# Moving half of one slot's scaling from VectorE to ScalarE, and the first pair of products behind the first half of the sums

## The chip, the cores and the metric

The kernel runs on one core of one Trainium2 chip. The metric is the time of one execution on the device, in microseconds. Engines are named as in the profile: PE is TensorE's matmul stream, PEld its weight loads, DVE is VectorE, ACT is ScalarE, POOL is GpSimd, SP is SyncE.

## The reference

A graph of 3,125 nodes and 103,125 edges goes through two graph layers, each with a residual and a layer norm. The first is a graph convolution; the change does not touch it. The second is an attention layer over edges with a message and an attention logit for each of 16 x 16 channels, and all that matters here is in these lines:

```
w_m = (efeat @ W_msg + b_msg).reshape(E, in_f, -1)
w_a = (efeat @ W_attn + b_attn).reshape(E, in_f, -1)
h_src = feat[src][:, :, None]
e1 = w_m * h_src
e2 = w_a * h_src
seg_max = segment_max(e2, dst)
ex = exp(e2 - seg_max[dst]);  denom = segment_sum(ex, dst)
ft = segment_sum(e1 * ex / denom[dst], dst).sum(axis=1)
```

## The kernel before

The second layer is the "edge part". Nodes lie 128 to a tile, one to a partition, in 25 tiles. The edges of a tile's nodes are handled in units: a unit takes 8 edges (slots 0 to 7) of each of the 128 nodes. A running maximum and running sums (`acc`) go from unit to unit; when a tile ends, its quotient is formed. There are 116 units, one after the other, and all engines run their own loop over them, four units to a pass, tied by semaphores.

For unit u the work is this. The weights of an edge are a product of its 16 features, split into bfloat16 terms, with a weight matrix: 8 slots x 512 columns of float32 in PSUM. `turn` (L789) transposes the terms on PE, in two halves; `turned` (L997) copies each half to SBUF on ACT. `product` k (L807), k = 0 to 3, makes the 512 columns of slots 2k and 2k+1. PSUM has room for four slots only (`pw`, four banks): products 0 and 2 write banks 0 and 1, products 1 and 3 write banks 2 and 3. Each slot's 512 columns are 16 blocks of 32, and block c is multiplied by channel c of the neighbour's features (`nbr`): that is the scaling, which empties PSUM into `eo`. DVE does it for slots 0 to 5 (`scaled`, L1471, three instructions of two slots); ACT does it for slots 6 and 7 (`last_pair`, L1021, one activation for each block, 32 in all). Then DVE takes the maximum (`peaks`, L1486 to L1505), ACT the exponential (`powers`, L1010), DVE multiplies (`weighted`, L1514), PE sums the 8 slots over an identity matrix in two halves (`sums`, L816 and L820), and DVE takes the sums out (`accumulate`, L1521).

The engines work on different units at a time. In one pass u,

- PE does: sums(u) first half; product 1 of unit u+3; sums(u) second half; turn half 0 of u+4; product 2 of u+3; turn half 1 of u+4; product 3 of u+3; product 0 of u+4.
- ACT does: `high` of u+4 (L982, L984); `last_pair` of u+2; `middle` of u+4 (L991); `fading` (L1002, L1004) and `powers` of u+1; `turned` halves 0 and 1 of u+4.
- DVE does: weighted(u); `rest_one` (L1452) of u+4; peaks of u+1, with the quotient of a tile that has ended (L1532 to L1541); `rest_two` (L1459) of u+4; scaled of u+3; accumulate(u).
- POOL gathers, as soon as `last_pair` of u+2 is done, the neighbours of unit u+6 (L626, eight indirect DMAs), and then the edge features of a later unit (L620).

The waits that matter: product 1 of u+3 waits for `last_pair` of u+2 (`s_pair1_act`), since both use banks 2 and 3; product 0 waits for the third instruction of `scaled` (`s_scaled`); product 2 waits for the first instruction of `scaled`; `last_pair` waits for product 3 (`s_w_act`).

Of the kernel before, what the change touches and what calls it, by code (L numbers as in the profile page):

```python
# [6 lines left out]
P = 128  # L7
# [6 lines left out]
ACT = mybir.ActivationFunctionType  # L14
# [5 lines left out]
FEAT = 16  # L20
HID = 64
CH = FEAT * FEAT
# [7 lines left out]
SETS = 4  # L30
RING = 4
LEAD = 4
# [28 lines left out]
def gnn_kernel(nc, x, src, dst, edge_attr, W1, b1, W2, b2, W3, b3, W_msg, b_msg, W_attn, b_attn, out):  # L61
# [9 lines left out]
    with ExitStack() as ctx:  # L71
        def sb(name, shape, dt=F32, stack=ctx):
            return stack.enter_context(nc.sbuf_tensor(name, shape, dt))

        def sem(name):
            return ctx.enter_context(nc.semaphore(name))
# [142 lines left out]
        nbr = sb("nbr", [P, SETS, SLOT * FEAT])  # L219
# [4 lines left out]
        eo = sb("eo", [P, RING, SLOT * 2 * CH])  # L224
# [14 lines left out]
        pw = ctx.enter_context(nc.psum_tensor("pw", [P, 4, 512], F32))  # L239
# [73 lines left out]
        s_settled_act = sem("s_settled_act")  # L313
# [4 lines left out]
        s_scaled = sem("s_scaled")  # L318
        s_attr = [sem(f"s_attr{b}") for b in range(SETS)]
        s_attr_ok = sem("s_attr_ok")  # L320
        s_attr_free = sem("s_attr_free")
# [6 lines left out]
        s_tT = sem("s_tT")  # L328
# [3 lines left out]
        s_pair0_free = sem("s_pair0_free")  # L332
        s_pair1_dve = sem("s_pair1_dve")
        s_pair1_act = sem("s_pair1_act")
        s_d = sem("s_d")
        s_ex = sem("s_ex")
        s_md = sem("s_md")
# [33 lines left out]
        block = ctx.enter_context(nc.Block())  # L371
# [268 lines left out]
        def _(pe):  # L640
# [117 lines left out]
            for layer in range(3):  # L758
# [4 lines left out]
                with pe.Fori(0, np_) as _p:  # L763
                    c = pe.snap(plane, min_val=0, max_val=MANY)
# [17 lines left out]
            def turn(unit, half, seen):  # L782

                if half == 0:
                    pe.wait_ge(s_lo, seen + 1)
                pe.wait_ge(s_tTc, seen * 2 + half + 1)
                pe.sem_inc(s_settled_pe, 1)
                for j in range(4):
                    mm = pe.matmul(pt[0:KROWS, j * P:(j + 1) * P], terms[:, unit, half * 4 + j, :], identb[:],  # L789
                                   start=True, stop=True)  # L790
                mm.then_inc(s_tT, 1)

            def product(unit, k, seen):

                pe.wait_ge(s_tTc, seen * 2 + k // 2 + 2)
                if k == 0:
                    pe.wait_ge(s_scaled, seen + SETS)
                elif k == 2:
                    pe.wait_ge(s_pair0_free, seen + 1)
                elif k == 1:  # L800
                    pe.wait_ge(s_pair1_act, seen + SETS)
                else:
                    pe.wait_ge(s_pair1_dve, seen + 1)
                pe.sem_inc(s_settled_pe, 1)
                for j in range(2):
                    lo = (2 * k + j) * P
                    mm = pe.matmul(pw[:, 2 * (k % 2) + j, :], termsT[:, unit, lo:lo + P], wk[:], start=True, stop=True)  # L807
                mm.then_inc(s_w_act if k == 3 else s_w, 1)

            def sums(ring, half, seen):  # L810

                total = pair[:, ring % 2, :]
                if half == 0:
                    pe.wait_ge(s_accd, seen + 1)
                    pe.sem_inc(s_settled_pe, 1)
                    pe.matmul(total, ident[:], acc[:], start=True, stop=False, skip_group_check=True)  # L816
                pe.wait_ge(s_p, seen * 2 + half + 1)
# [11 lines left out]
            for u in range(3):  # L829
                for half in range(2):  # L830
                    turn((u + 1) % 2, half, u + 1)
                for k in range(4):
                    product(u % 2, k, u)
            product(1, 0, 3)
            before_last = pe.value_load(levels[0:1, NT + 1:NT + 2], min_val=1, max_val=MANY)

            def pe_unit(b, u, ahead):

                sums(b % RING, 0, u)
                if ahead > 2:  # L840
                    product((b + 3) % 2, 1, u + 3)
                sums(b % RING, 1, u)
                if ahead > 3:
                    turn(b % 2, 0, u + LEAD)
                if ahead > 2:
                    product((b + 3) % 2, 2, u + 3)
                if ahead > 3:
                    turn(b % 2, 1, u + LEAD)
                if ahead > 2:
                    product((b + 3) % 2, 3, u + 3)  # L850
                if ahead > 3:
                    product(b % 2, 0, u + LEAD)

            with pe.Fori(0, before_last) as i:
                for b in range(SETS):
# [5 lines left out]
        def _(act):  # L861
# [71 lines left out]
            for layer in range(3):  # L933
# [8 lines left out]
                with act.Fori(0, np_) as _p:  # L942
                    c = act.snap(plane, min_val=0, max_val=MANY)
# [67 lines left out]

            def last_pair(ring, held, seen):

                act.wait_ge(s_nbr_ok, seen + 1)
                act.wait_ge(s_w_act, seen + 1)
                act.sem_inc(s_settled_act, 1)
                wide = 2 * FEAT
                for j in range(SLOT - 2, SLOT):
                    for c in range(FEAT):
                        lo = j * 2 * CH + c * wide  # L1020
                        done = act.activation(eo[:, ring, lo:lo + wide], pw[:, j - 4, c * wide:(c + 1) * wide], ACT.Copy,  # L1021
                                              scale=nbr[:, held, j * FEAT + c:j * FEAT + c + 1])
                done.then_inc(s_pair1_act, 1)

            act.wait_ge(s_stage, 1)
# [39 lines left out]
        def _(dve):  # L1065
# [10 lines left out]
                      s_g3_free, s_accd):  # L1076
                dve.sem_inc(s, 1)
            dve.sem_inc(s_g3, 2)
            for s in (s_scaled, s_attr_free, s_tT, s_pair1_act):
                dve.sem_inc(s, 4)  # L1080
            dve.sem_inc(s_tTc, 1)
            dve.sem_inc(s_recw, 16)
# [272 lines left out]
            for layer in range(3):  # L1355
# [8 lines left out]
                with dve.Fori(0, np_) as p:  # L1364
                    c = dve.snap(plane, min_val=0, max_val=MANY)
# [44 lines left out]
            wide = [P, NG, FEAT]  # L1410
# [53 lines left out]
            def scaled(ring, held, seen):  # L1464

                dve.wait_ge(s_nbr_ok, seen + 1)
                for k in range(3):
                    dve.wait_ge(s_w, seen * 3 + k + 1)
                    dve.sem_inc(s_settled_dve, 1)
                    h_src = nbr[:, bass.ds(held, 1), 2 * k * FEAT:(2 * k + 2) * FEAT].rearrange("p u c -> p (u c)")  # L1470
                    dve.tensor_tensor(eo[:, bass.ds(ring, 1), k * 4 * CH:(k + 1) * 4 * CH]  # L1471
                                      .rearrange("p r (c f) -> p (r c) f", f=2 * FEAT),
                                      pw[:, 2 * (k % 2):2 * (k % 2) + 2, :].rearrange("p b (c f) -> p (b c) f", f=2 * FEAT),
                                      h_src.unsqueeze(2).broadcast_to([P, 2 * FEAT, 2 * FEAT]),
                                      ALU.mult).then_inc((s_pair0_free, s_pair1_dve, s_scaled)[k], 1)

            def peaks(ring, first, old, new, seen, ended=None):
# [184 lines left out]
```

## Time and profile before

| what | value |
|---|---|
| three timed runs | 2610.61, 2631.48, 2644.78 us; median 2631.48 us |
| span of the profiled execution | 2618.5 us (13 us under the median) |
| mean granted TensorE clock over the span | 0.897 |
| PE, DVE, ACT, POOL busy | 72%, 76%, 56%, 49% of the span |
| first and last `accumulate` of the edge part | 905.9 and 2589.8 us |

The span is the only time of the profiled execution itself, and it lies within the spread of the timed runs. A unit of the edge part takes on average (2589.8 - 905.9) / 114 = 14.8 us.

### The profile page before, as it was taken

Reading aid. Unit: us, or ns where it says so; the run is one execution under the profiler, and the core shown is the slowest. Engines: PE = TensorE matmul, PEld = TensorE weight load, DVE = VectorE, ACT = ScalarE, POOL = GpSimd, SP = SyncE. Lnnn points to the kernel's source line nnn. Section 1 sums busy time; section 2 is a strip of 40 time slices with the busy share of each in tenths; the row PEclk is TensorE's granted clock in tenths of the full one; section 3 lists DMA queues with packets and bytes.
Section 4 is the critical chain, followed back from the end, with each engine's and each line's share of the span. In section 5 each row is a group of like instructions: output and inputs, shape, how many; then the busy total and the mean of one; then the engine's idle time right before and its main releaser. Section 6 shows DMA issues by size and latency. Waiting matters only on the chain.

```text
span 2618.5 us, 37987 instructions
## 1 busy us (share of the span) xinstructions
PE 1880.0 (72%) x5814; PEld 706.3 (27%) x5815; DVE 1989.2 (76%) x3269; ACT 1458.7 (56%) x4999; POOL 1289.6 (49%) x1520
## 2 busy tenths in 40 slices
PE   2445676577982577787887777877888877888855
PEld 1111111132341133233333333333333333333322
DVE  5678999752011588888888888888898898988866
ACT  5124444210001576676777767777776776776643
POOL 2200000425556566656666657666666665666650
PEclk9789989788975699999999989999998998998877
DMA  2000000000001000000000000000000000000000
GB/s 31 17 23 4 0 0 0 2 10 17 11 13 15 9 10 10 9 10 9 10 9 10 9 10 9 10 9 10 9 10 9 10 10 9 9 10 9 9 5 7
DMA packets 85243, 25.74 MB, mean 10 GB/s; under 512 B 61677, under 2 KB 82271, under 8 KB 85087
## 3 DMA queue, kind: packets, MB, share of 16 engines
q0 software_dynamic: 36672, 18.09, 5.7%
q1 hardware_dynamic: 48463, 6.91, 1.8%
q10 hardware_dynamic: 80, 0.43, 0.1%
q14 instruction: 18, 0.15, 0.0%
q8 instruction: 10, 0.16, 0.0%
HBM read 22.73 MB, written 2.51 MB: 10 GB/s over the span
## 4 chain that ended last, share of the span: by engine, by line
issue 29%; DVE 25%; PE 23%; DVEq 17%; ACT 3%; POOL 1%; another core or an unknown queue 1%; DMA 1%; ACTq 0%; POOLq 0%; PEldq 0%; PEld 0%
PE pair L820 9%; DVE eo L1471 6%; DVE hot L1197 4%; DVEq L1490 4%; PE pw L711 3%; DVE eo L1514 2%; DVE eo L1505 2%; PE pw L807 2%; PE pw L708 2%; PE pw L707 2%; DVE top L1486 2%; ACT eo L1021 2%; DVE top L1491 2%; DVE bank L1499 2%; DVEq L1503 1%
## 5 line engine op out<-in xcount | busy, mean ns | idle before, releaser
L626 POOL DMA_INDIRECT nbr<-table,rec x928 | 961.0, 1036 | 527.3 <-ACT eo L1021 274.0
L820 PE MATMUL pair<-eo,ident 128*128 128x512 f32 x1856 | 890.0, 625 | 12.4 <-issue 7.7
L1021 ACT ACTIVATE eo<-pw,nbr 128x32 f32<-128x32 f32 x3712 | 694.3, 371 | 83.1 <-issue 66.9
L1471 DVE TENSOR_TENSOR eo<-pw,nbr 128x1024 f32 (+1 forms) x348 | 412.5, 1218 | 169.3 <-PE pw L807 94.4
L820 PEld LDWEIGHTS pair<-eo,ident 128*128 128x128 f32 x1856 | 366.2, 201 | 494.9 <-issue 479.6
L807 PE MATMUL pw<-wk,termsT 100*128 100x512 bf16 x928 | 307.5, 417 | 249.8 <-issue 173.8
L1197 DVE TENSOR_SCALAR hot<-iota_key,near_key 128x500 bf16<-128x500 f16 x974 | 273.8, 346 | 59.3 <-issue 31.9
L1010 ACT ACTIVATE eo<-eo 128x2048 f32<-128x2048 f32 x116 | 221.5, 1910 | 107.4 <-DVE eo L1505 85.1
L1514 DVE TENSOR_TENSOR eo<-eo x232 | 272.7, 1216 | 5.9 <-issue 4.0
L1505 DVE TENSOR_TENSOR eo<-eo,bank (+1 forms) x116 | 265.3, 2287 | 10.7
L672 PE MATMUL bank<-hot 128*128 128x500 bf16 x488 | 146.7, 414 | 145.4 <-DVE hot L1197 93.1
L997 ACT CAST termsT<-pt 100x512 bf16<-100x512 f32 x232 | 135.5, 584 | 207.3 <-issue 123.4
L789 PE MATMUL pt<-identb,terms 128*100 128x128 bf16 x928 | 99.4, 234 | 171.2 <-issue 83.1
L672 PE MATMUL pair<-hot,x 128*128 128x500 bf16 x474 | 138.3, 412 | 63.5 <-DVE hot L1197 60.4
L807 PEld LDWEIGHTS pw<-wk,termsT 100*128 100x128 bf16 x928 | 68.3, 101 | 409.9 <-issue 409.1
L620 POOL DMA_INDIRECT attr<-in_edge_attr_dram,rec x116 | 115.5, 995 | 98.2 <-issue 57.6
L1486 DVE TENSOR_TENSOR top<-eo 128x1024 f32 (+1 forms) x116 | 141.4, 1219 | 28.2 <-issue 28.2
L789 PEld LDWEIGHTS pt<-identb,terms 128*100 128x100 bf16 x928 | 78.2, 135 | 299.1 <-issue 299.1
L816 PE MATMUL pair<-acc,ident 128*128 128x512 f32 x232 | 145.3, 712 | 5.9 <-DVE acc L1521 4.6
L553 POOL TENSOR_SCALAR place<-place 128x25 f32<-128x25 f32 x1 | 0.4, 387 | 280.9 <-ACTq L958 280.9
L900 ACT CAST counts<-bank 128x500 f32 x79 | 45.5, 576 | 156.0 <-PEq L695 123.8
L900 ACT CAST counts<-pair 128x500 f32 x79 | 45.5, 576 | 141.6 <-PEq L695 130.6
(245 smaller groups left out, 1815.6 us busy)
## 6 DMA issues: line engine op xcount, KB each, us to landing
nbr<-table,rec POOLq DMA_INDIRECT x928
rec<-unit_recs SPq DMA_DIRECT2D x116, 8.0 KB
attr<-in_edge_attr_dram,rec POOLq DMA_INDIRECT x116
unit_recs<-place SPq DMA_DIRECT2D x27, 64.0 KB
shared<-key_row SPq DMA_DIRECT2D x1, 1600.0 KB, 6.7
counts<-in_dst_dram SPq DMA_DIRECT2D x1, 448.0 KB
counts<-in_src_dram SPq DMA_DIRECT2D x1, 448.0 KB
place<-in_src_dram,at_i POOLq DMA_INDIRECT x26, 2.6
```

What stands on the lines that cost most here:

```text
L626: pool.indirect_dma_start(nbr[:, b, j * FEAT:(j + 1) * FEAT], None, table, bass.IndirectOffsetOnAxis(ap=rec[:, b, j:j + 1], axis=0)).then_ ...
L672: return pe.matmul(bank[v][:, 0:NG * WIN], low, hot_key[:, k, :], start=first, stop=False, skip_group_check=True)
L789: mm = pe.matmul(pt[0:KROWS, j * P:(j + 1) * P], terms[:, unit, half * 4 + j, :], identb[:], start=True, stop=True)
L807: mm = pe.matmul(pw[:, 2 * (k % 2) + j, :], termsT[:, unit, lo:lo + P], wk[:], start=True, stop=True)
L820: mm = pe.matmul(total, ident[:], eo[:, ring, j * 2 * CH:(j + 1) * 2 * CH], start=False, stop=(j == SLOT - 1), skip_group_check=True)
L1010: act.activation(here, here, ACT.Exp).then_inc(s_ex, 1)
L1021: done = act.activation(eo[:, ring, lo:lo + wide], pw[:, j - 4, c * wide:(c + 1) * wide], ACT.Copy, scale=nbr[:, held, j * FEAT + c:j * FE ...
L1197: return dve.tensor_scalar(hot_key[:, slot, :].rearrange("p (a d) -> p a d", a=NG), iota_key[:], near_key[v][:, k], None, ALU.is_equal)
L1471: dve.tensor_tensor(eo[:, bass.ds(ring, 1), k * 4 * CH:(k + 1) * 4 * CH] .rearrange("p r (c f) -> p (r c) f", f=2 * FEAT), pw[:, 2 * (k % ...
L1486: dve.tensor_tensor(wide(top4[:]), attention(ring, 0, 4), attention(ring, 4, 8), ALU.max).then_inc(s_attr_free, 1)
L1505: dve.tensor_tensor(here, here, wide(after).unsqueeze(1).broadcast_to([P, SLOT, FEAT, FEAT]), ALU.subtract).then_inc(s_d, 1)
L1514: dve.tensor_tensor(here, here, attention(ring, 4 * half, 4 * half + 4), ALU.mult).then_inc(s_p, 1)
```

## The change

ACT also scales the second half of slot 5 (blocks 8 to 15, from bank 1), ahead of its 32 blocks for slots 6 and 7, and signals that with a new semaphore, `s_half_act`. DVE's third scaling instruction covers one and a half slots in place of two. Product 0 of unit u+3 now also has to wait for ACT's half (banks 0 and 1), and it is moved: from the end of pass u-1 to pass u, between the first half of the sums and product 1. The prologue's extra `product(1, 0, 3)` goes.

```diff
             def product(unit, k, seen):
                 pe.wait_ge(s_tTc, seen * 2 + k // 2 + 2)
                 if k == 0:
                     pe.wait_ge(s_scaled, seen + SETS)
+                    pe.wait_ge(s_half_act, seen + SETS)
...
-            product(1, 0, 3)
...
                 sums(b % RING, 0, u)
                 if ahead > 2:
+                    product((b + 3) % 2, 0, u + 3)
                     product((b + 3) % 2, 1, u + 3)
...
-                if ahead > 3:
-                    product(b % 2, 0, u + LEAD)
...
             def last_pair(ring, held, seen):
+                def block(j, c):
+                    lo = j * 2 * CH + c * wide
+                    return act.activation(eo[:, ring, lo:lo + wide], pw[:, j - 4, c * wide:(c + 1) * wide], ACT.Copy,
+                                          scale=nbr[:, held, j * FEAT + c:j * FEAT + c + 1])
                 act.wait_ge(s_nbr_ok, seen + 1)
+                act.wait_ge(s_scaled, seen + SETS + 1)
+                act.sem_inc(s_settled_act, 1)
+                for c in range(FEAT // 2, FEAT):
+                    done = block(5, c)
+                done.then_inc(s_half_act, 1)
                 act.wait_ge(s_w_act, seen + 1)
                 act.sem_inc(s_settled_act, 1)
                 for j in range(SLOT - 2, SLOT):
                     for c in range(FEAT):
-                        ...
+                        done = block(j, c)
                 done.then_inc(s_pair1_act, 1)
...
                 for k in range(3):
+                    blocks = 2 * FEAT if k < 2 else 3 * FEAT // 2
...
-                                      h_src.unsqueeze(2).broadcast_to([P, 2 * FEAT, 2 * FEAT]),
+                                      h_src.unsqueeze(2).broadcast_to([P, blocks, 2 * FEAT]),
                                       ALU.mult).then_inc((s_pair0_free, s_pair1_dve, s_scaled)[k], 1)
```

## Rows read from the trace of the kernel before

**Rows 1.** The page: busy time by engine, and the chain that ended last

```profile
PE 1880.0 (72%) x5814; PEld 706.3 (27%) x5815; DVE 1989.2 (76%) x3269; ACT 1458.7 (56%) x4999; POOL 1289.6 (49%) x1520
...
issue 29%; DVE 25%; PE 23%; DVEq 17%; ACT 3%; POOL 1%; another core or an unknown queue 1%; DMA 1%; ACTq 0%; POOLq 0%; PEldq 0%; PEld 0%
```

**Rows 2.** Timeline of PE in one pass: start, us, line, operation [idle before]

```profile
1812.11 3.67 PE L820 MATMUL pair<-eo,ident 128*128 128x512 f32 x8
1817.76 0.59 PE L807 MATMUL pw<-wk,termsT 100*128 100x512 bf16 x2 [1.98 <-issue]
1818.19 3.60 PE L820 MATMUL pair<-eo,ident 128*128 128x512 f32 x8
1821.62 0.39 PE L789 MATMUL pt<-identb,terms 128*100 128x128 bf16 x4
...
1822.86 0.40 PE L789 MATMUL pt<-identb,terms 128*100 128x128 bf16 x4 [0.41 <-ACT termsT L997]
...
1824.10 0.59 PE L807 MATMUL pw<-wk,termsT 100*128 100x512 bf16 x2 [0.41 <-issue]
```

**Rows 3.** Timeline of ACT in the same pass, to the next last_pair

```profile
1810.65 5.23 ACT L1021 ACTIVATE eo<-pw,nbr 128x32 f32<-128x32 f32 x28
1816.12 0.82 ACT L1021 ACTIVATE eo<-pw,nbr 128x32 f32<-128x32 f32 x4 [0.24 <-issue]
...
1822.13 0.59 ACT L997 CAST termsT<-pt 100x512 bf16<-100x512 f32 x1 [0.77 <-PE pt L789]
...
1824.56 4.92 ACT L1021 ACTIVATE eo<-pw,nbr 128x32 f32<-128x32 f32 x27
```

**Rows 4.** Timeline of DVE in the same pass: the third scaling instruction

```profile
1822.72 1.23 DVE L1471 TENSOR_TENSOR eo<-pw,nbr 128x1024 f32 x1 [0.93 <-issue]
```

**Rows 5.** Costliest groups: L1021 and L1471 by the page, L1491 by shape

```profile
L1021 ACT ACTIVATE eo<-pw,nbr 128x32 f32<-128x32 f32 x3712 | 694.3, 371 | 83.1 <-issue 66.9
L1471 DVE TENSOR_TENSOR eo<-pw,nbr 128x1024 f32 (+1 forms) x348 | 412.5, 1218 | 169.3 <-PE pw L807 94.4
...
L1491 DVE TENSOR_TENSOR top<-top 128x512 f32<-128x512 f32 x62 | 42.9, 692 | 5.5
```

**Rows 6.** Timeline of POOL: a gather of edge features

```profile
1829.39 0.95 POOL L620 DMA_INDIRECT attr<-in_edge_attr_dram,rec  x1 [0.30 <-issue]
```

**Rows 7.** Timeline of a pass with a tile's end, and the next

```profile
1848.26 0.42 ACT L1002 ACTIVATE mdiff<-mdiff 128x256 f32<-128x256 f32 x1 [3.64 <-DVE mdiff L1501]
...
1850.97 0.40 PE L789 MATMUL pt<-identb,terms 128*100 128x128 bf16 x4 [2.52 <-DVE terms L1459]
...
1855.01 5.82 ACT L1021 ACTIVATE eo<-pw,nbr 128x32 f32<-128x32 f32 x32
...
1861.06 0.60 PE L807 MATMUL pw<-wk,termsT 100*128 100x512 bf16 x2
...
1865.51 0.57 ACT L997 CAST termsT<-pt 100x512 bf16<-100x512 f32 x1
```

**Rows 8.** How often a tile ended and a unit was accumulated

```profile
L1532 DVE RECIPROCAL rden<-pair x25: 1748/1750/1758, 1009.7 to 2599.2; 128x256 f32 x25
...
L1521 DVE TENSOR_TENSOR acc<-pair,fade x115: 677/680/690, 905.9 to 2589.8; 128x512 f32<-128x512 f32 x115
```

**Rows 9.** Timeline of PE in two passes with slow second halves; windows (PEclk eighth)

```profile
1874.67 0.59 PE L807 MATMUL pw<-wk,termsT 100*128 100x512 bf16 x2 [1.87 <-issue]
1875.11 5.29 PE L820 MATMUL pair<-eo,ident 128*128 128x512 f32 x8
...
2415.31 1.01 PE L807 MATMUL pw<-wk,termsT 100*128 100x512 bf16 x2 [3.34 <-ACT eo L1021]
2416.12 6.18 PE L820 MATMUL pair<-eo,ident 128*128 128x512 f32 x8
...
2415.30:2422.30 7.00, 6.99 (x13) 2.96 (x14) 3.23 (x4) 2.69 (x4) 4.82 (x5) 0.57 0.06 5
```

More of the change, by code:

```diff
@@ L334, in gnn_kernel @@
         s_pair1_act = sem("s_pair1_act")
+        s_half_act = sem("s_half_act")
         s_d = sem("s_d")
@@ L1012, in last_pair @@
             def last_pair(ring, held, seen):
-                act.wait_ge(s_nbr_ok, seen + 1)
+                wide = 2 * FEAT
+                def block(j, c):
+                    lo = j * 2 * CH + c * wide
+                    return act.activation(eo[:, ring, lo:lo + wide], pw[:, j - 4, c * wide:(c + 1) * wide], ACT.Copy,
+                                          scale=nbr[:, held, j * FEAT + c:j * FEAT + c + 1])
+                act.wait_ge(s_nbr_ok, seen + 1)
+                act.wait_ge(s_scaled, seen + SETS + 1)
[3 more added lines that the diff above has]
+                done.then_inc(s_half_act, 1)
                 act.wait_ge(s_w_act, seen + 1)
                 act.sem_inc(s_settled_act, 1)
-                wide = 2 * FEAT
                 for j in range(SLOT - 2, SLOT):
                     for c in range(FEAT):
-                        lo = j * 2 * CH + c * wide
-                        done = act.activation(eo[:, ring, lo:lo + wide], pw[:, j - 4, c * wide:(c + 1) * wide], ACT.Copy,
-                                              scale=nbr[:, held, j * FEAT + c:j * FEAT + c + 1])
+                        done = block(j, c)
                 done.then_inc(s_pair1_act, 1)
@@ L1078, in _ @@
             dve.sem_inc(s_g3, 2)
-            for s in (s_scaled, s_attr_free, s_tT, s_pair1_act):
+            for s in (s_scaled, s_attr_free, s_tT, s_pair1_act, s_half_act):
                 dve.sem_inc(s, 4)
@@ L1469, in scaled @@
                     dve.sem_inc(s_settled_dve, 1)
-                    h_src = nbr[:, bass.ds(held, 1), 2 * k * FEAT:(2 * k + 2) * FEAT].rearrange("p u c -> p (u c)")
-                    dve.tensor_tensor(eo[:, bass.ds(ring, 1), k * 4 * CH:(k + 1) * 4 * CH]
+                    blocks = 2 * FEAT if k < 2 else 3 * FEAT // 2
+                    h_src = nbr[:, bass.ds(held, 1), 2 * k * FEAT:2 * k * FEAT + blocks].rearrange("p u c -> p (u c)")
+                    dve.tensor_tensor(eo[:, bass.ds(ring, 1), k * 4 * CH:k * 4 * CH + blocks * 2 * FEAT]
                                       .rearrange("p r (c f) -> p (r c) f", f=2 * FEAT),
-                                      pw[:, 2 * (k % 2):2 * (k % 2) + 2, :].rearrange("p b (c f) -> p (b c) f", f=2 * FEAT),
-                                      h_src.unsqueeze(2).broadcast_to([P, 2 * FEAT, 2 * FEAT]),
+                                      pw[:, 2 * (k % 2):2 * (k % 2) + 2, :].rearrange("p b (c f) -> p (b c) f", f=2 * FEAT)
+                                      [:, 0:blocks, :],
+                                      h_src.unsqueeze(2).broadcast_to([P, blocks, 2 * FEAT]),
                                       ALU.mult).then_inc((s_pair0_free, s_pair1_dve, s_scaled)[k], 1)
```

## The prediction

> **What bounds the kernel now.** The page comes first. DVE is the busiest engine and ACT the least loaded of the three that matter; the chain that ended last gives more to DVE than to PE and almost nothing to ACT [rows 1]. Read by shares alone, work should go from DVE to ACT, and 44% idle on ACT looks like room. That is an average, so I read the timelines of one ordinary pass, engine by engine, and asked at each idle stretch what it waited for. On PE, the first half of the sums ends at 1812.11 + 3.67 = 1815.78, and then PE sits idle for 1.98 us until product 1 starts at 1817.76 [rows 2]. By the code product 1 waits for `last_pair`. The records of ACT's 32 activations end at 1816.94 with a short hole, and `last_pair` runs from 1810.65, so product 1 comes 7.11 us after its start [rows 3]. In 34 of the 111 passes that I could measure this way, product 1 comes 5.9 to 6.2 us after the start, and the 32 activations then run without a hole in 5.82 us [rows 7]. In the other passes there are holes of about 0.25 to 1.1 us in or just behind `last_pair`, and they come with the gather of edge features, which POOL issued at 1829.39, 4.83 us after the next `last_pair` began [rows 3, 6].
>
> From product 1 the path goes on without a gap: second half of the sums at 1818.19, turn half 0 at 1821.62 [rows 2], its copy on ACT at 1822.13 [rows 3], turn half 1 at 1822.86 [rows 2], its copy, `high`, and the next `last_pair` at 1824.56 [rows 3]. So ACT and PE form a ring: 7.11 us of `last_pair` and 6.80 us from product 1 to the next `last_pair`, 13.91 us together, which is the period. DVE is not on it: it waits 0.93 us in this pass for product 2, which stands behind the sums on PE [rows 4]. The chain of waits enters DVE because that wait is short, not because DVE sets the pace.
>
> Two kinds of pass differ. In one that ends a tile DVE has the quotient to do, ACT waits 3.64 us for the maximum and PE 2.52 us for DVE's terms [rows 7]: DVE bounds it. In the pass after it the ring has slack: `last_pair` starts at 1855.01, product 1 at 1861.06 straight behind PE's late sums, and the copy at 1865.51 starts straight behind the exponential, with no idle time [rows 7]. There are 25 tile ends, 24 of them in the loop, and 116 units [rows 8]; that leaves some 66 ordinary passes, 24 with a tile's end, 24 behind one.
>
> **The change part by part.**
>
> *ACT gets 8 activations more in `last_pair`.* Gapless, 32 take 5.82 us and the last one about 0.3, so one comes every (5.82 - 0.3) / 31 = 0.178 us [rows 7]; by the page's busy sum, 694.3 / 3712 = 0.187 us [rows 5]. Eight cost 1.43 to 1.50 us. The new wait and settle step between the blocks of slot 5 and of slot 6 waits for something long done (product 3) but breaks the overlap of two activations: 0 to 0.2 us, I take 0.1. Together 1.55 us. In an ordinary pass all of it lies on the ring, since product 1 waits for the last block: 66 x 1.55 = 102 us. Behind a tile's end product 1 would come at 1855.01 + 5.92 + 1.55 = 1862.5, 1.4 us later than now, of which some 0.1 is slack behind the exponential: 24 x 1.3 = 31 us. In a tile's pass the cover is DVE's quotient, 2.52 us on PE: 0. If that cover were gone, 24 x 1.55 = 37 us more.
>
> *ACT's 1.3 us of idle time elsewhere doesn't pay for it.* ACT's idle 0.77 us stands before the copy of half 0 [rows 3], where it waits for PE, which waits for `last_pair`. Lengthening one moves the other.
>
> *DVE's third scaling instruction shrinks from 1024 to 768 columns.* 1024 take 1.218 us and an operation of 512 takes 0.692 [rows 5], so 0.26 us goes. It comes off DVE's stretch, which already waits 0.93 us in ordinary passes [rows 4]; it is worth something only in the tile passes, 24 x 0.26 = 6 us.
>
> *ACT's new wait for `s_scaled`.* The scaling ends at 1822.72 + 1.23 = 1823.95 and `last_pair` starts at 1824.56 [rows 3, 4]: 0.6 us to spare, 0.87 with the shorter instruction. Queued behind it on ACT are everything from `last_pair` on; at nothing now, 0.1 to 0.3 us a pass if the signal were late.
>
> *Product 0 moves.* It leaves its place at 1824.10, where it stood before the sums, and goes to 1815.78, into PE's idle stretch [rows 2]. Its two matmuls fill 0.4 to 0.6 of it and cost nothing. Its new wait, for ACT's half, is met 1.5 us after `last_pair` starts, over 3 us before PE gets there; queued behind it are product 1 and the second half of the sums. DVE needs it only for the first scaling instruction, long after. It was not on the ring before, so its going brings nothing back. No DMA is moved; POOL's gathers follow `last_pair`'s end and so shift with it.
>
> *PE's clock.* The second half of the sums normally takes 3.60 us. In 20 of 113 passes it takes 5.0 to 6.2, and the stretch with 6.18 has a mean granted clock of 0.57, most of it at 1.2 instead of 2.4 GHz [rows 9]. What PE did before tells which: with less than 1.8 us idle ahead of product 1, none of 41 was slow; 1.8 to 2.3 us, 6 of 47, one of them behind 1.87 us [rows 9]; 2.3 to 2.6, 7 of 17; over 2.6, 7 of 8, three of them behind 3.3 us or more with 6.2 us, such as the one at 2415.31 [rows 9]. These counts are over the whole loop, passes of all three kinds. The change makes the idle stretch longer by 1.55 and fills 0.5 of it with product 0: from about 2.1 to 3.1 us wherever `last_pair` has holes. So most such passes turn slow, at 1.7 us (5.29 - 3.60) to 2.6 us (6.18 - 3.60). But a slow pass delays the next `last_pair` against POOL's gathers; behind the one at 2415.31 it had no hole (5.92 us), which makes the next pass 1.2 us shorter and its sums fast. I take two of three ordinary passes slow, 44 at 2.0 us = 88 us, less the 20 at 1.9 us = 38 that are slow already: +50 us. Bounds: 0 (the share stays) and +94 (all 66 at 2.0, less 38).
>
> The Trainium skill, page "TensorE: Matmul & The Clock Gate", section "HAM oscillation — how this bites in real kernels", says that a wait in every pass of a loop can send the array back to the cold clock each time, so that the warm-up is paid in every pass. By that rule the upper bound holds; the counts above lean to it and don't reach it.
>
> The Trainium skill's page "ScalarE: Activation LUTs", section "What ACT_TABLE_LOAD costs", gives 186 ns + 0.833 ns for each element, 93 ns more for a pointer operand, and 93 ns of overlap. An estimate from it is 213 ns for a block of 32 with a pointer scale, 1.70 us for eight; the rows say 0.178 to 0.187, and the measurement decides. The sum would be 18 us higher by the page.
>
> **Sum.** 102 + 31 - 6 + 50 = 177 us on the profile's 2618.5, so 2795 for a span like that one. The median lies 13 us above the span; I add it here and in every rival, and get 2808, say 2810 us, 6.8% slower.
>
> **The rivals.**
>
> *Clock indifferent:* the share of slow sums stays, 127 us: 2760. For it: of the 64 passes with 1.8 to 2.6 us of idle only 13 are slow, so idle time alone doesn't decide. Against: the 7 of 8.
>
> *Every ordinary pass slow, and slow second halves reach past the 2.52 us of cover in tile passes:* 102 + 31 + 94 and 24 x 1.2 = 29: +256, 2888. For it: the rule above. Against: the passes without holes that follow a long one.
>
> *The holes go.* They depend on where the gather falls. If the 40 activations ran without one (7.4 us in place of 7.11), an ordinary pass would grow by 0.3 us: 66 x 0.3 + 31 = 51, 2683, within 2%. Against: `last_pair`'s end itself starts the gathers, so they keep their distance to the next one, and a longer `last_pair` reaches further into them.
>
> *The other side: DVE is the bound,* as its share of the chain says, and ACT's addition vanishes in its 44% idle. Then each pass gains 0.26 us: 116 x 0.26 = 30, 2601 us. It decides if product 1 starts before `last_pair`'s end or if DVE has no wait for product 2. Against: the 0.93 us on DVE and the 1.98 us on PE.
>
> *It doesn't do what it says:* if the half block's wait held product 0 and the sums behind it, the cost would be above the forecast, not below; with 3 us to spare I give it nothing.
>
> **How the numbers follow.** Forecast (2775 to 2855) 0.50; clock indifferent 0.20; every pass slow 0.15; holes go 0.09; DVE the bound 0.04; anything else 0.02. Leaving out the last three and the far end of the third: 2735 to 2885. About 2% (53 us) is what can be told from no change, as the runs before spread over 34 us. Slower by over 2%: the first three and a small half of the fourth, 0.89; within 2%: 0.09; faster: 0.02.
>
> **What would show it.** In the profile after, ordinary passes should show product 1 at 8.6 to 8.9 us behind the start of `last_pair`, still straight at its end; DVE's wait before the third scaling instruction grown from 0.9 to over 2 us; product 0 right behind the first half of the sums without a wait; an idle stretch of about 3 us before product 1; slow second halves in more than half of the ordinary passes; tile passes near 16.5 us. An ordinary period still near 13.9 us would prove the ring wrong; product 1 waiting for anything but `last_pair`, or a hole-free `last_pair`, would make the time too high; slow sums in tile passes too would make it too low.

## The result and the profile after

The kernel with the change takes 2812.53 us (median of 4 runs, 2804.88 to 2823.65) against 2628.47 us before (4 runs, 2610.61 to 2644.78): a ratio of 1.0717 [1.0659, 1.0775], 7% slower. The profiled execution has a span of 2821.8 us at a mean granted clock of 0.882. Some executions fall into a second, slower state (four of the ten of e12 below), and all ratios here are taken without them.

From the first to the last `accumulate` the edge part now takes 2793.1 - 921.8 = 1871.3 us, against 1683.9: +187.4 of the 203 us between the spans. The other 16 us lie outside it, 12 of them already there at an activation ahead of the edge part (L974, 800.36 us before, 812.35 after), in code that the change doesn't touch; a second profile of the same kernel (e9 below) has only 8 of them.

The page of the kernel after, its busy times, its chain and two of its groups (busy us, mean ns | idle before, and what ended most of it), beside [rows 1, 5]:

```profile
PE 1929.7 (68%) x5814; PEld 737.9 (26%) x5815; DVE 1970.9 (70%) x3269; ACT 1615.0 (57%) x5927; POOL 1293.5 (46%) x1520
...
PE 43%; issue 31%; DVE 8%; ACT 8%; DVEq 6%; POOL 1%; DMA 1%; PEldq 0%; ACTq 0%; POOLq 0%; another core or an unknown queue 0%; PEld 0%
...
L1019 ACT ACTIVATE eo<-pw,nbr 128x32 f32<-128x32 f32 x4640 | 861.8, 363 | 100.1 <-issue 85.4
L1482 DVE TENSOR_TENSOR eo<-pw,nbr 128x1024 f32 (+1 forms) x348 | 382.9, 1131 | 313.7 <-PE pw L809 188.0
```

DVE's scaling lost 30 us (412.5 to 382.9) and nearly doubled its waits for the products, 169.3 to 313.7 us. ACT took 156 us more and its share of the span stands still, since the span grew with it. The chain has moved from DVE (25%) to PE (43%).

The timeline of PE after, in two ordinary passes that follow each other (start, us, line and operation [idle before]):

```profile
1762.27 3.67 PE L822 MATMUL pair<-eo,ident 128*128 128x512 f32 x8
1765.78 0.60 PE L809 MATMUL pw<-wk,termsT 100*128 100x512 bf16 x2
1768.45 0.59 PE L809 MATMUL pw<-wk,termsT 100*128 100x512 bf16 x2 [2.07 <-issue]
1768.88 3.60 PE L822 MATMUL pair<-eo,ident 128*128 128x512 f32 x8
...
1779.76 0.60 PE L809 MATMUL pw<-wk,termsT 100*128 100x512 bf16 x2
1784.41 0.68 PE L809 MATMUL pw<-wk,termsT 100*128 100x512 bf16 x2 [4.06 <-issue]
1784.89 5.25 PE L822 MATMUL pair<-eo,ident 128*128 128x512 f32 x8
```

ACT and DVE in the same two passes:

```profile
1761.12 7.23 ACT L1019 ACTIVATE eo<-pw,nbr 128x32 f32<-128x32 f32 x40
...
1775.05 4.45 ACT L1019 ACTIVATE eo<-pw,nbr 128x32 f32<-128x32 f32 x24
1780.46 0.46 ACT L1019 ACTIVATE eo<-pw,nbr 128x32 f32<-128x32 f32 x2 [0.95 <-issue]
1781.19 0.29 ACT L1019 ACTIVATE eo<-pw,nbr 128x32 f32<-128x32 f32 x1 [0.27 <-issue]
1781.89 2.42 ACT L1019 ACTIVATE eo<-pw,nbr 128x32 f32<-128x32 f32 x13 [0.42 <-issue]
```

```profile
1773.41 0.96 DVE L1482 TENSOR_TENSOR eo<-pw,nbr 128x768 f32 x1 [1.45 <-issue]
...
1784.89 0.29 DVE L1469 TENSOR_TENSOR terms<-res,terms 128x128 f32 x1 [1.42 <-ACT terms L991]
...
1791.07 0.96 DVE L1482 TENSOR_TENSOR eo<-pw,nbr 128x768 f32 x1 [3.24 <-PE pw L809]
```

In the first pass the 40 activations run without a hole in 7.23 us, product 0 stands right behind the first half of the sums, product 1 comes 0.10 us behind `last_pair`'s end, and the second half of the sums takes 3.60 us. In the second, `last_pair` has 1.64 us of holes and ends 9.26 us after its start; PE is idle 4.06 us, and the sums behind it take 5.25 us. DVE waits 1.45 us in one and 3.24 us in the other, where [rows 4] had 0.93.

Averages over the loop (the first two columns by the starts of `accumulate`, the others from the timelines, between the same instructions as in [rows 2, 3]), in us; "slow" counts the passes in which the second half of the sums takes 4.6 us or more, where the others take 3.6 (the last of the 113 passes, slow after the change, has no turn behind it and isn't in the table):

| pass | period before, after | `last_pair`, with holes | product 1 behind its end | product 1 to turn 0 | slow |
|---|---|---|---|---|---|
| ordinary | 14.34, 16.08 | 6.86, 8.25 | 0.29, 0.10 | 4.34, 4.96 | 16, 40 of 65 |
| behind a tile's end | 13.64, 16.76 | 5.87, 8.11 | 0.17, 0.10 | 4.03, 5.26 | 2, 17 of 23 |
| with a tile's end | 17.08, 16.99 | 6.29, 8.29 | 0.20, 0.11 | 6.36, 5.56 | 2, 19 of 23 |

66 x 1.74 = 115 us, 24 x 3.12 = 75 and 24 x (-0.09) = -2: together the 188 us of the edge part.

### The profile page after: what moved, and what is told of

It is laid out like the page before. It is cut to its first block, busy times and chain, and to the rows that moved or that the text cites. A ratio compares the mean times of both kernels' runs of the same rounds, so it can differ in the third digit from the quotient of the medians.

```text
span 2821.8 us, 39065 instructions
## 1 busy us (share of the span) xinstructions
PE 1929.7 (68%) x5814; PEld 737.9 (26%) x5815; DVE 1970.9 (70%) x3269; ACT 1615.0 (57%) x5927; POOL 1293.5 (46%) x1520
## 4 chain that ended last, share of the span: by engine, by line
PE 43%; issue 31%; DVE 8%; ACT 8%; DVEq 6%; POOL 1%; DMA 1%; PEldq 0%; ACTq 0%; POOLq 0%; another core or an unknown queue 0%; PEld 0%
PE pair L822 24%; PE pw L809 6%; ACT eo L1019 5%; DVE hot L1207 3%; PE pair L818 3%; PE pw L712 3%; PE pw L709 2%; PE pt L790 2%; PE pw L708 2%; ACT eo L1010 1%; POOL shared L531 1%; ACT termsT L997 1%; DVEq L1502 1%; PE bank L673 1%; DVEq L1203 1%
## 5 line engine op out<-in xcount | busy, mean ns | idle before, releaser
L822 PE MATMUL pair<-eo,ident 128*128 128x512 f32 x1856 | 974.6, 674 | 15.7 <-DVE eo L1526 11.7
L1019 ACT ACTIVATE eo<-pw,nbr 128x32 f32<-128x32 f32 x4640 | 861.8, 363 | 100.1 <-issue 85.4
L1482 DVE TENSOR_TENSOR eo<-pw,nbr 128x1024 f32 (+1 forms) x348 | 382.9, 1131 | 313.7 <-PE pw L809 188.0
L809 PE MATMUL pw<-wk,termsT 100*128 100x512 bf16 x928 | 299.0, 406 | 369.7 <-issue 368.6
L822 PEld LDWEIGHTS pair<-eo,ident 128*128 128x128 f32 x1856 | 397.4, 219 | 555.4 <-issue 540.8
L809 PEld LDWEIGHTS pw<-wk,termsT 100*128 100x128 bf16 x928 | 74.3, 99 | 496.2 <-issue 495.8
L818 PE MATMUL pair<-acc,ident 128*128 128x512 f32 x232 | 132.6, 654 | 88.5 <-issue 77.9
L790 PE MATMUL pt<-identb,terms 128*100 128x128 bf16 x928 | 93.1, 224 | 115.2 <-issue 66.4
```

The lines of the kernel that those rows point to most:

```text
L1019: return act.activation(eo[:, ring, lo:lo + wide], pw[:, j - 4, c * wide:(c + 1) * wide], ACT.Copy, scale=nbr[:, held, j * FEAT + c:j * FE ...
L1482: dve.tensor_tensor(eo[:, bass.ds(ring, 1), k * 4 * CH:k * 4 * CH + blocks * 2 * FEAT] .rearrange("p r (c f) -> p (r c) f", f=2 * FEAT), p ...
```

## The experiments

The kernel before was run beside each of them on the same chip. It took 2716 us on the chip of e1 to e4, 2713 us on that of e5 to e8 and 2626 us on that of e9 to e12, so ratios are compared, and profiles of e1 to e8 with e5, not with [rows 1 to 9]. "Edge" is the time from the first to the last `accumulate`.

### What the change's parts do: e1, e2, e3, e5, e9

**e1: product 0 is moved, ACT scales 32 blocks as before.**

```diff
-            product(1, 0, 3)
...
                 if ahead > 2:
+                    product((b + 3) % 2, 0, u + 3)
                     product((b + 3) % 2, 1, u + 3)
...
-                if ahead > 3:
-                    product(b % 2, 0, u + LEAD)
```

> The kernel before with product 0 moved behind the first half of the sums and nothing else (DVE scales all of slots 0 to 5, ACT only slots 6 and 7). Ring theory (last_pair on ACT, then product 1, second half of the sums and turn on PE set the pass): product 0 was never on the ring and now fills idle time of PE, so the time stays within 1% of before (2600 to 2645 us), perhaps 10 to 30 us faster if a shorter idle stretch leaves fewer slow second halves than the 20 of 113. Rival (the move itself costs, since product 1 and the sums now queue behind product 0's waits): over 2% slower, some 0.6 us a pass, 2700 us.

Measured: 2722.59 us, 1.003 [0.9995, 1.0066]; edge 1789.8 against 1780.1 in e5. The move is free, and it brings nothing.

**e2: before, with eight more activations of 32 columns, into a spare tile, in front of `last_pair`'s signal.** **e3: the same eight behind the signal.**

```diff
                         done = act.activation(eo[:, ring, lo:lo + wide], ...)
+                for c in range(FEAT // 2):
+                    done = act.activation(spare[:, c * wide:(c + 1) * wide], ident[...], ACT.Copy, scale=dinv[:, c:c + 1])
                 done.then_inc(s_pair1_act, 1)
```

> The kernel before with 8 additional activations of 32 columns (scaled copies of the identity into a spare tile that nobody reads) at the end of last_pair, in front of its signal; no change on PE or DVE. Ring theory: the ring grows by 1.45 us a pass, plus the clock's reaction to the longer idle stretch of PE (here about 3.6 us, longer than in the changed kernel as product 0 doesn't fill any of it), so at least as slow as the changed kernel: 2790 to 2850 us. Rival (the slowdown comes from product 0's new place or from ACT's new wait for the scaling): under 2700 us.

> The same 8 additional activations, but behind last_pair's signal. ACT's load is that of the run with them in front. Ring theory: product 1 starts as early as before; ACT has about 1.5 to 2 us of idle time between last_pair and the copy of half 0 in an ordinary pass and much more in a tile's pass, so most of it is hidden: within 2% of before, 2620 to 2680 us. Rival (ACT's total load is what counts): as slow as with them in front, 2790 us or more.

Measured: e2 2987.58 us, 1.1036 [1.0963, 1.1109], edge 2037.7; e3 2753.93 us, 1.0181 [1.0118, 1.0243], edge 1804.5. One pass of e2 on PE, then on ACT:

```profile
1817.05 3.67 PE L821 MATMUL pair<-eo,ident 128*128 128x512 f32 x8
1824.79 1.01 PE L808 MATMUL pw<-wk,termsT 100*128 100x512 bf16 x2 [4.07 <-ACT spare L1025]
1825.59 6.27 PE L821 MATMUL pair<-eo,ident 128*128 128x512 f32 x8
```

```profile
1821.08 1.89 ACT L1022 ACTIVATE eo<-pw,nbr 128x32 f32<-128x32 f32 x10 [0.22 <-issue]
1822.80 1.85 ACT L1025 ACTIVATE spare<-ident,dinv 128x32 f32<-128x32 f32 x8
```

And one of e3 on ACT, where product 1 came at 1829.60, before the eight were done:

```profile
1827.62 1.89 ACT L1022 ACTIVATE eo<-pw,nbr 128x32 f32<-128x32 f32 x10 [0.28 <-issue]
1829.33 1.84 ACT L1026 ACTIVATE spare<-ident,dinv 128x32 f32<-128x32 f32 x8
```

The same work on the same engine costs 271 us in front of the signal and 38 us behind it. So it is `last_pair`'s end that PE waits for, not ACT's load. 271 us are 2.3 us a pass, more than the 1.7 us by which the eight put product 1 off (it comes 1.78 us behind the last of `last_pair`'s own activations in ordinary passes, in e5 0.12). The rest goes with the second halves: nearly all are slow in e2 (109 of 113, e5 42), 5.03 us on the mean against 4.20. I had expected e2 at 2790 to 2850 us where before takes 2628, a ratio of at most 1.085; it is worse than that. In e2 product 0 doesn't stand in the idle stretch as it does in the change; that this is why e2 costs more than the change is only argued.

**e5 and e9: the kernel before, and the kernel after, once more.** No edit.

> The kernel before, unchanged, for its profile on the chip that ran the others of this set. Both theories expect the pattern of the first profile: product 1 at last_pair's end, about 20 of 113 second halves slow. If this chip is one on which the kernel before takes 2716 us, the profile should show where the 3% come from; I expect longer holes in ACT's stream around last_pair.

> The changed kernel, unchanged, timed and profiled on the chip of the others of this set, so that the runs with its variants can be compared part by part. Expected: the ratio of 1.07 again. If this is the kind of chip on which the kernel before takes some 2715 us, its last_pair should be longer than the 8.25 us of the first profile of the changed kernel, as the holes in ACT's stream were longer there in the kernel before too.

Measured: e5 2721.82 us (one run), edge 1780.1; e9 2812.74 us, 1.0708 [1.0661, 1.0755], edge 1878.7. e9 repeats the result: 40 of 65 ordinary passes slow again, `last_pair` 8.31 us there, product 1 0.10 us behind its end. e5 is the profile that e1 to e8 are read against: an ordinary pass of 15.12 us, `last_pair` 7.08, 42 of 113 second halves slow. That is twice the 20 that I expected on this chip too; the longer `last_pair` came as expected.

### What the wait on PE costs, and the clock: e4, e7, e12, e6

**e4: before, the second half of the sums in front of product 1.** **e7: after, the same swap (in front of products 0 and 1).**

```diff
+                sums(b % RING, 1, u)
                 if ahead > 2:
                     product((b + 3) % 2, 1, u + 3)
-                sums(b % RING, 1, u)
```

> The kernel before with the second half of the sums put in front of product 1, so that PE does it while last_pair still runs. Ring theory: product 1 then starts at the later of last_pair's end and the sums' end (about 8.8 us after last_pair's start) and turn half 0 follows at once, some 1.6 us earlier than now; the pass falls from 13.9 us to DVE's own 12.7 to 12.8, and the slow second halves cost nothing as PE is not idle for long: 66 x 1.1 + 38 = about 110 us less, 2510 to 2550 us. Rival (DVE is what bounds ordinary passes, and its wait for product 2 is only its other side): no change, 2600 to 2640 us.

> The changed kernel with the second half of the sums in front of products 0 and 1. Ring theory: the 7.3 us of 40 gapless activations end before PE is through with both halves of the sums (about 8.8 us after last_pair's start), so the longer last_pair is hidden wherever it has few holes; the pass falls to that of the kernel before with the sums first (ratio 0.98), within 0.01 to 0.03 above it because the holes reach past the cover: 0.98 to 1.01 against before. Rival (the loss is not on product 1's path): stays at 1.07.

Measured: e4 2648.15 us, 0.9805 [0.9724, 0.9886], edge 1701.6; e7 2791.65 us, 1.0301 [1.0247, 1.0356], edge 1845.4. Both fall short of what I expected (0.955 to 0.97, and 0.98 to 1.01). PE in two passes of e4, then ACT's waits from 1000 to 2500 us in e4 and from 1000 to 2600 us in e7 (us in total, times, longest):

```profile
1814.14 7.03 PE L820 MATMUL pair<-eo,ident 128*128 128x512 f32 x16
1821.01 0.60 PE L807 MATMUL pw<-wk,termsT 100*128 100x512 bf16 x2
...
1838.89 1.91 PE L816 MATMUL pair<-acc,ident 128*128 128x512 f32 x2
1840.59 7.26 PE L820 MATMUL pair<-eo,ident 128*128 128x512 f32 x16
```

```profile
ACT eo L1021 <- issue: 180.3, 344, 3.3
```

```profile
ACT eo L1019 <- issue: 253.8, 474, 1.2
```

There is no idle stretch between the halves, and no second half is slow. The swap takes over half of the change's loss back, 1.07 to 1.03, and makes the kernel before faster. It doesn't win the clock back, though: the slow matmuls move to the start of the pass. Its first half (two matmuls of `acc`, L816, and eight of the sums) takes more than 5.3 us, where the others take 4.8, in 67 of 114 passes of e4 and 104 of e7, against 13 in e5 and 6 in the kernel after; the second pass shown has one, with 1.91 us for the two `acc` matmuls, which take 1.10 elsewhere. Both halves together take 9.17 us on the mean in e4 and 9.14 in e5, and the mean granted clock falls to 0.849 in e4 and 0.826 in e7, from 0.895 in e5. So what is won is that the second half of the sums no longer stands behind `last_pair`. Part of it goes again by holes in `last_pair`: 344 waits of ACT in 1500 us of e4, where e5 has 169, and 474 in 1600 us of e7, where the kernel after, on its chip, has 134.

**e12: before, order of a pass: both halves of the sums, turn half 0, products 1 and 2, turn half 1, product 3, product 0.**

```diff
+                sums(b % RING, 1, u)
+                if ahead > 3:
+                    turn(b % 2, 0, u + LEAD)
                 if ahead > 2:
                     product((b + 3) % 2, 1, u + 3)
-                sums(b % RING, 1, u)
-                if ahead > 3:
-                    turn(b % 2, 0, u + LEAD)
-                if ahead > 2:
                     product((b + 3) % 2, 2, u + 3)
```

> The kernel before with PE's order changed to: first and second half of the sums, turn half 0, then product 1, product 2, turn half 1, product 3, product 0. Against e4 (ratio 0.98) the turn and its copy no longer wait for last_pair, which takes about 1 us more off the ring; the next last_pair still needs product 3, which needs product 1. Ring theory: ordinary passes with long holes fall by up to 1 us more, the others stay on DVE's 12.8: a ratio of 0.955 to 0.98. Rival (e4's gain was all there is, the rest being holes and signals from elsewhere): 0.98, or above.

Measured: 2634.9 us (median of all ten runs), 0.9998 [0.9964, 1.0032], edge 1694.3: a miss for my theory. PE's and ACT's waits in it, 1000 to 2500 us:

```profile
PE pt L789 <- DVE terms L1458: 87.6, 48, 5.0
```

```profile
ACT eo L1020 <- issue: 151.7, 278, 3.2
```

The turn, pulled ahead, waits for DVE's terms, 87.6 us in 48 passes, `last_pair` has holes as in e4, and the first half of the sums is slow in 76 of 114 passes (19 in the kernel before), at a mean granted clock of 0.852. e4 and e12 differ in their order and in their chip, so whether e4's 2% would also stand on the chip of e12 is open.

**e6: after, with product 0 computed five times over, to keep PE at work while it waits.**

```diff
-                for j in range(2):
+                for j in range(2) if k else [0, 1] * 5:
```

> The changed kernel with product 0 computed five times over (the same result, the signal behind the last), which fills about 1.7 us of the 2 to 4 us in which PE idled ahead of product 1. Nothing on ACT or DVE changes and product 1 still has to wait for last_pair. Clock theory (most of the second halves are slow because of the idle stretch): most of them go back to 3.6 us and the time falls by 50 to 100 us against the changed kernel, to a ratio of 1.03 to 1.05 to before. Rival (the slow second halves come from elsewhere, or are hidden): no fall, a ratio of 1.07 or more, as the repeats only load PE.

Measured: 2901.58 us, 1.0701 [1.0644, 1.0759], edge 1941.6: as slow against its before as the change itself, a miss. A pass on PE:

```profile
1811.11 2.32 PE L809 MATMUL pw<-wk,termsT 100*128 100x512 bf16 x10
1816.30 0.59 PE L809 MATMUL pw<-wk,termsT 100*128 100x512 bf16 x2 [2.87 <-issue]
1816.73 3.60 PE L822 MATMUL pair<-eo,ident 128*128 128x512 f32 x8
```

Slow second halves are 45 of 113, where the kernel after has 77 on its chip, but the fall is behind a tile's end (4 of 23 slow, after 17) and in tile passes (6 of 23, after 19). Of the ordinary passes 35 of 65 stay slow: `last_pair` takes 9.25 us there, by more holes, and PE is still idle 2.46 us ahead of product 1 on the mean. The ten matmuls are hardly ever on the path themselves: product 1 stands 0.10 us behind `last_pair`'s end in ordinary passes and 0.14 behind a tile's end. Passes behind a tile's end do get shorter, 15.93 us against 16.76, and ordinary ones longer, 17.28 against 16.08. So e6 doesn't isolate the clock. As the unchanged kernel after has no profile on that chip, whether the filler or the chip brought the further holes is open.

### The holes in `last_pair`: e11

**e11: after, with one neighbour gather per unit in place of eight, the other slots filled once with a constant.**

```diff
-                    for j in range(SLOT):
+                    for j in range(1):
                         pool.indirect_dma_start(nbr[:, b, j * FEAT:(j + 1) * FEAT], None, table, ...)
```

> The changed kernel with only one of the eight neighbour gathers of each unit (the other seven slots keep a constant, so the result is wrong in them by design of the run: the work is left out). POOL's stretch of gathers behind last_pair shrinks from 11 us to about 2.5. If the holes in ACT's stream come with the gathers, last_pair falls to 7.2 to 7.4 us in nearly all passes, the idle stretch of PE to 2 us, and the slow second halves from 77 to 20 or fewer: 2640 to 2700 us on the faster kind of chip, a ratio of 1.00 to 1.03. If the holes come from ACT's own stream of instructions, last_pair stays at 8.2 us and the ratio near 1.07.

Measured: 2581.56 us (two runs), 0.9843 [0.9796, 0.9891], edge 1667.5; 25 us of the gain on the kernel before lie ahead of the edge part, which starts at 880.4 us. I had expected 1.00 to 1.03. ACT's waits inside `last_pair` in the kernel after, then in e11 (1000 to 2600 us), and one pass of e11 on ACT, POOL and PE:

```profile
ACT eo L1019 <- issue: 64.7, 134, 1.1
```

```profile
ACT eo L1021 <- issue: 2.3, 5, 0.9
```

```profile
1809.59 7.22 ACT L1021 ACTIVATE eo<-pw,nbr 128x32 f32<-128x32 f32 x40
1811.78 1.01 POOL L623 DMA_INDIRECT attr<-in_edge_attr_dram,rec  x1 [7.17 <-DMA rec<-unit_recs]
```

```profile
1814.29 0.60 PE L811 MATMUL pw<-wk,termsT 100*128 100x512 bf16 x2
1816.91 0.59 PE L811 MATMUL pw<-wk,termsT 100*128 100x512 bf16 x2 [2.02 <-issue]
1817.34 3.60 PE L824 MATMUL pair<-eo,ident 128*128 128x512 f32 x8
```

Without the gathers the holes are gone: `last_pair` takes 7.22 us in ordinary passes and behind a tile's end alike. With that the idle stretch is 2.02 us, the sums behind it are fast in this pass, and slow second halves fall from 77 to 29 of 113, not to the 20 or fewer that I expected: 7 of 65 in ordinary passes, but 14 of 23 behind a tile's end, with the same idle stretch (2.04 and 2.09 us on the mean). So the length of that stretch isn't all that decides; what else does is open. An ordinary pass takes 14.13 us with 40 activations, 1.95 us less than in the kernel after: 1.03 by the holes and 0.91 by the clock. The holes come with the neighbour gathers. The gather of edge features, which e11 keeps and which falls into `last_pair` as shown, makes none by itself. Whether the holes come through POOL's issuing or through the transfers isn't told apart.

### The other way: less on ACT, e8 and e10

**e8: before, with DVE taking the first half of slot 6 in a fourth instruction; ACT scales 24 blocks, slot 7 first.** **e10: before, with that half left out.**

```diff
-                for j in range(SLOT - 2, SLOT):
-                    for c in range(FEAT):
+                for j in (SLOT - 1, SLOT - 2):
+                    if j == SLOT - 2:
+                        act.wait_ge(s_half_dve, seen + SETS + 1)
+                        act.sem_inc(s_settled_act, 1)
+                    for c in range(FEAT // 2 if j == SLOT - 2 else 0, FEAT):
```

The new instruction waits for product 3 and stands ahead of `accumulate` on DVE; product 1 and POOL's gathers wait for it too. So e8 changes more than ACT's load.

> The opposite of the change, on the kernel before: DVE takes the first half of slot 6 in a fourth, 256-column instruction, and ACT scales 24 blocks (slot 7, then the rest of slot 6). Ring theory: 1.43 us off the ring in an ordinary pass, and PE's idle stretch shrinks, so fewer slow second halves; DVE gets 0.43 us more, which bounds the pass at about 13.1 us and costs 0.43 us in each pass with a tile's end and behind it. Sum about -0.7 x 66 - 38 + 20 = -60 us, a ratio of 0.97 to 0.985. Rival (DVE bounds the kernel): 116 x 0.43 = 50 us slower, 1.02.

> The kernel before with 8 of ACT's 32 activations left out (the first half of slot 6 is not scaled by anyone, and that part of the result is stale); DVE and PE unchanged. It takes 1.43 us off last_pair and adds nothing anywhere, so it shows whether the ring works in both directions, without the fourth DVE instruction that e8 had. Ring theory: ordinary passes fall from 14.3-15.1 to DVE's 12.8 to 13.3 us, as last_pair then ends before the gathers' holes begin, and slow second halves go with the idle stretch: 60 to 130 us less than before, a ratio of 0.95 to 0.98. Rival (something else, such as signals from PE, sets the pass as in e8): no gain or a loss.

Measured: e8 2894.36 us, 1.068 [1.0624, 1.0736], edge 1944.3; e10 2682.67 us, 1.0221 [1.0181, 1.026], edge 1740.2. Both are misses: I expected a gain. Waits in e8, then in e10, from 1000 to 2500 us:

```profile
ACT termsT L999 <- remote: 166.8, 52, 4.9
...
DVE eo L1483 <- remote: 155.5, 60, 5.5
```

```profile
POOL attr L620 <- DMA rec<-unit_recs: 136.4, 26, 6.8
ACT termsT L997 <- remote: 108.2, 18, 7.8
...
DVE eo L1472 <- remote: 81.9, 18, 7.5
```

And a pass of e8 on DVE and PE:

```profile
1810.24 0.42 DVE L1483 TENSOR_TENSOR eo<-pw,nbr 128x256 f32 x1 [5.45 <-remote]
...
1811.43 2.05 PE L818 MATMUL pair<-acc,ident 128*128 128x512 f32 x2 [5.91 <-DVE acc L1534]
1813.27 4.79 PE L822 MATMUL pair<-eo,ident 128*128 128x512 f32 x8
```

In e8 `last_pair` is free of holes (4.38 us) and one second half of 113 is slow. But ACT's second copy and DVE's fourth instruction wait up to 4.9 and 5.5 us for something that the profile shows no source of ("remote"), 52 and 60 times in 1500 us, more often than every second pass. PE waits behind them for `accumulate`, and the first half of the sums then runs slow in 112 of 114 passes: 6.77 us on the mean against 4.94 in e5, 209 us in all, where the edge part grew by 164. The slow clock has moved from the second half to the first, and the mean granted clock is 0.82. e8 is no test of the ring, then. In e10 most passes do get shorter (ordinary median 13.54 us against 13.90), but a few stand for 5 to 8 us, and POOL waits 136 us for record loads, where the kernel before has 23.2 us of that wait in 9 passes. So the kernel before lies close to a second limit, which shorter passes run into. That limit reads like the records' loads in e10. In e8 POOL waits 107.3 us for them, 30 times, where e5 has 27.8 us and 9; whether they are the source there too is open.

## Why the prediction was right

*The ring held.* Product 1 stands 0.10 us behind `last_pair`'s end in every kind of pass, DVE's and ACT's idle time bought nothing, e1 shows the move at no cost, and e2 against e3 shows that place and not load decides. The rival "DVE is the bound" falls by that and by DVE's waits, up from 169 to 314 us.

*Eight more activations.* Put at 1.43 to 1.50 us; a gapless `last_pair` went from 5.82 to 7.2 us, 1.4. Ordinary passes grew by 1.39 in `last_pair`, less 0.19 because product 1's delay behind it shrank, where I had 1.55: 79 us, predicted 102. The holes in ordinary passes stayed what they were, 8.25 - 7.2 = 1.05 us after, 6.86 - 5.82 = 1.04 before, as the argument on POOL's distance said; "the holes go" falls with that. That they come with the gather of edge features was misread: e11 keeps that gather and has no hole.

*Behind a tile's end: the term that was mis-sized.* I took +1.3 us and no change of the clock, 31 us; it was +3.1, 75 us. `last_pair` grew by 2.24 there and not by 1.4. It doesn't reach further into the gathers; they come closer to its start. In a tile's pass `last_pair` ends 2 us later (8.29 us behind its start in place of 6.29), POOL starts its gathers that much later, and DVE's cover keeps the pass as long as it was. So the next `last_pair` starts 9.54 us behind that end, where it had 11.74, and the eighth neighbour gather is issued 0.62 us after its start on the mean and no longer 0.87 before it. One such pass on POOL before (its `last_pair` starts at 1855.01 [rows 7]), and one on POOL and ACT after:

```profile
1854.35 0.94 POOL L626 DMA_INDIRECT nbr<-table,rec  x1 [0.30 <-issue]
```

```profile
1742.90 1.33 POOL L627 DMA_INDIRECT nbr<-table,rec  x1 [0.30 <-issue]
1742.97 1.53 ACT L1019 ACTIVATE eo<-pw,nbr 128x32 f32<-128x32 f32 x8
1745.56 5.79 ACT L1019 ACTIVATE eo<-pw,nbr 128x32 f32<-128x32 f32 x32 [1.05 <-issue]
```

Of the 29 holes in these 23 passes, 24 begin in the first 5.87 us, where the 32 activations of before also stood with 2 holes in all; and 15 of them, 8.8 of 17.1 us, stand right behind the eighth block, at the new wait and settle step, which I had put at 0.1 us. What that step waits for, product 3, was done 0.7 to 2.3 us before `last_pair` began in each of them; e9 shows 11 more, and e11, without the gathers, none. "They keep their distance" holds where the ring sets the pass, and I hadn't asked what it means behind a pass that DVE sets. The clock is the other part: 17 of 23 second halves are slow where 2 were, 1.23 us on the mean. The idle stretch ahead of product 1 grew there from 0.79 to 3.35 us, since PE no longer comes late; the holes are not the whole reason, as 14 of 23 are slow in e11 too.

*The clock.* Slow second halves went from 20 to 77 of 113. In ordinary passes 40 of 65 are slow, predicted 44 of 66; the cost there is 66 x 0.62 = 41 us, predicted 50. (Of the 20 that the prediction takes off there, 16 stand in ordinary passes. It also left out first halves, of which 19 of 114 were slow before and 6 after.) Behind a tile's end it adds 24 x 1.23 = 30, predicted nothing. By PE's idle time ahead of product 1, not counting product 0's own, 60 of 66 passes with 2.6 us or more were slow, 12 of 25 with 2.3 to 2.6, 4 of 17 with 1.8 to 2.3 and none of 4 with less: the prediction's split carries over, and with 3 us or more 52 of 53 were slow. "Clock indifferent" falls. "Every pass slow" falls too: the pass at 1761 keeps 3.60 us behind 2.07 us of idle time. The Trainium skill, page "TensorE: Matmul & The Clock Gate", section "HAM oscillation — how this bites in real kernels", describes a loop whose wait for a DMA in each pass brings a cold start each time; this trace agrees for 40 of 65 ordinary passes and not for the others.

*Tile passes:* -0.1 us, predicted 0 with DVE's -6 us in all; the whole is 24 x 0.09 = 2. Slow sums came here too, in 19 of 23 passes where 2 were. The prediction had named that as a sign that its time would be too low; it wasn't one, as the passes stayed at 16.99 us: DVE's cover held.

*The sum:* ordinary 115 (predicted 152), behind a tile's end 75 (31), tile passes -2 (-6): 188 against 177. Two misses of some 40 us with opposite signs met, so the closeness of 2810 to 2812.5 is partly luck; and the 16 us outside the edge part are cancelled by the offset between span and median, 13 us one way before and 9 us the other way after.

*The signs named.* Product 1 was to come 8.6 to 8.9 us behind `last_pair`'s start: the mean over the ordinary passes is 8.35, and it is two cases, 38 passes under 8.0 and 23 over 9.2, such as 7.33 and 9.36 in the rows above. DVE's wait, "over 2 us", is 2.6 on the mean, and the idle stretch, "about 3 us", 3.1; they too mix two cases, like 1.45 and 3.24, and 2.07 and 4.06. Product 0 without a wait and slow halves in over half of the ordinary passes came as said. Not foreseen: ACT's `middle` comes later, so DVE's `rest_two` waits for it, 1.42 us in the pass shown; DVE then waits 3.24 us more for product 2, so this costs nothing.

## What to carry to other kernels

Before work goes from the busiest engine to an idle one, look at where in the idle engine's order it would stand: the same eight activations cost 10% in front of a signal that another engine waits for and 2% behind it. A wait in the middle of PE's pass costs more than its length once the clock falls behind it. Moving ready matmuls in front of the waiting ones takes them off the path, which was worth 2% in one order and nothing in another; look afterwards at where the slow matmuls are, as here they only moved. Where passes differ in kind, apply each argument to each kind, and ask what one kind hands to the next: a stretch that is clean today may be clean only because the pass ahead of it is long.

## What the runs showed of the hardware that I had not expected

- ScalarE's stream of small activations has holes of some 0.2 to 1.1 us while indirect gathers are under way: 134 of them (64.7 us) in 1.6 ms with eight gathers a unit, 5 (2.3 us) with one. Behind a tile's end half of that time stands at a wait for a product that had been done over 2 us before.
- Slow matmuls move rather than go: with the sums in one block the second half was never slow, but the first half was in 67 of 114 passes (13 in the kernel before, e5), and the granted clock fell from 0.895 to 0.849 while the kernel got 2% faster.
- Shorter passes can be slower ones: with 8 of 32 activations left out, the median ordinary pass fell by 0.36 us and the kernel took 2.2% longer, by stalls of 5 to 8 us in 18 passes.
- Work that only kept TensorE busy (ten matmuls, 2.32 us) went with 45 of 113 slow second halves in place of 77 (on another chip) and won no time.
- The same kernel took 2626 us on one chip and 2713 to 2716 us on two others, 3% apart.
